# Causal attention: row maxima from full banks, one mask per diagonal bank, two weighted sums in a row

## The reference, cut to what matters

```
x: (8, 1024, 256)                          # batch, positions, features; 16 heads of 16
q, k, v = einsum('bte,hed->bhtd', x, Wq), ... Wk, ... Wv
scores  = einsum('bhtd,bhsd->bhts', q, k)
scores  = where(causal, scores, -inf) / sqrt(256)
w       = softmax(scores, axis=-1)
out     = einsum('bhts,bhsd->bhtd', w, v)
```

## Time and profile before

| | us |
|---|---|
| median of 3 runs | 5277.7 |
| lowest and highest | 5261.9, 5290.58 |
| the profiled execution, whole | 5293.36 |
| its span | 5291.6 |

### The profile page before, as it was taken

How to read it: one execution, slowest core, us unless ns; L and a number is a source line. 1 busy time by engine, 2 the same in 40 slices (tenths; PEclk the granted TensorE clock), 3 DMA queues, 4 the chain that set the end, 5 groups by cost and what they waited for, 6 DMA issues and landing times. The chain is left out here.

```text
span 5291.6 us, 68269 instructions
## 1 busy us (share of the span) xinstructions
PE 4637.5 (88%) x23444; PEld 2457.6 (46%) x23444; DVE 3439.4 (65%) x6212; ACT 2705.4 (51%) x3205; POOL 1377.1 (26%) x1043
## 2 busy tenths in 40 slices
PE   5999999999976888888888888888878999999999
PEld 3544444444433544455445544555543444444443
DVE  5566566656647888878887888455545565565653
ACT  1444444445453344443444344122227888888888
POOL 1011111111112332233233332000004545455454
PEclk7787778778787998999899899999989999999999
DMA  6233222322310000000000000000016766666664
GB/s 166 60 74 64 73 62 62 86 62 72 72 37 15 0 0 0 0 0 0 0 0 0 0 0 0 13 1 0 0 31 156 162 153 144 162 146 154 152 146 110
DMA packets 145900, 322.06 MB, mean 61 GB/s; under 512 B 39504, under 2 KB 64480, under 8 KB 129264
## 3 DMA queue, kind: packets, MB, share of 16 engines
q1 hardware_dynamic: 137664, 310.88, 25.6%
q10 hardware_dynamic: 7920, 7.87, 0.5%
q0 software_dynamic: 64, 0.05, 0.0%
HBM read 237.93 MB, written 80.74 MB: 60 GB/s over the span
## 5 line engine op out<-in xcount | busy, mean ns | idle before, releaser
L1714 ACT ACTIVATE gelu_out<-hidden,b_col 128x1024 f32<-128x1024 f32 x1024 | 1085.4, 1111 | 171.1 <-PE hidden L1628 169.9
L529 ACT ACTIVATE probsT<-scoresT 128x1024 f32<-128x1024 f32 (+3 forms) x768 | 603.8, 810 | 609.7 <-PE scoresT L467 603.9
L577 DVE TENSOR_REDUCE maxima<-front 128x1 f32<-128x512 f32 (+3 forms) x1280 | 735.7, 630 | 274.4 <-PE front L439 177.7
L1694 POOL TENSOR_TENSOR combined<-combined,gated 128x512 f32<-128x512 f32 x480 | 615.6, 1283 | 679.0 <-DVE gated L1812 679.0
L918 POOL TENSOR_TENSOR pair_sums<-sims 128x1024 f32<-128x1024 f32 x256 | 487.9, 1913 | 1140.0 <-DVE pair_exp L1032 777.3
L1812 DVE SCALAR_TENSOR_TENSOR gated<-expert_out,b_col,gates_spread 128x512 f32<-128x512 f32 x480 | 359.1, 748 | 452.1 <-PE expert_out L1638 246.7
L1628 PE MATMUL hidden<-slice_stack,w_stack 128*128 128x512 f32 x2048 | 626.9, 428 | 14.1 <-ACT gelu_out L1714 14.1
L433 PE MATMUL front<-k_stack,q_stack 48*128 48x512 f32 (+3 forms) x1536 | 541.3, 493 | 62.2 <-DVE maxima L577 35.6
L1638 PE MATMUL expert_out<-gelu_out,w_sb 128*32 128x512 f32 x4096 | 547.2, 606 | 31.1 <-DVE gated L1812 26.0
L379 POOL TENSOR_SCALAR_AFFINE_SELECT probsT<-probsT 128x512 f32<-128x512 f32 x256 | 164.7, 644 | 1383.0 <-ACT probsT L529 1383.0
L1628 PEld LDWEIGHTS hidden<-slice_stack,w_stack 128*128 128x128 f32 x2048 | 353.2, 189 | 368.5 <-ACT gelu_out L1714 278.8
(11 more groups left out here) (188 smaller groups left out, 6389.8 us busy)
## 6 DMA issues: line engine op xcount, KB each, us to landing
gates_spread<-gate_scratch SPq DMA_DIRECT2D x512, 256.0 KB, 4.9
stack_scratch<-split_parts SPq DMA_DIRECT2D x192, 256.0 KB, 3.1
slice_stack<-slice_scratch SPq DMA_DIRECT2D x128, 256.0 KB, 7.9
q_stack<-stack_scratch SPq DMA_DIRECT2D x64, 384.0 KB, 6.4
k_stack<-stack_scratch SPq DMA_DIRECT2D x64, 384.0 KB, 9.5
slice_scratch<-slice_parts SPq DMA_DIRECT2D x32, 512.0 KB, 6.3
x_tiles<-in_L_attn_x SPq DMA_DIRECT2D x8, 1024.0 KB, 11.8
out_x<-x_tiles ACTq DMA_DIRECT2D x15, 512.0 KB, 4.7
```

The lines of the kernel that those rows point to most:

```text
L529: nc.scalar.activation(PT[:, i % NPT, 2 * pr:2 * pr + 2, at:BANK], ST[pr][:, :, at:BANK], ACT.Exp, scale=SCALE).then_inc(probs_ready, 1)
L577: nc.vector.tensor_reduce(dst, F[k % 3][:, 0:parts * w].rearrange("p (a k) -> p a k", a=parts), AX.X, ALU.max)\
L1694: nc.gpsimd.tensor_tensor(CM[:, par, hc, :], CM[:, par, hc, :], Y[:, u % 2, :], ALU.add)\
L1714: nc.scalar.activation(GH[:, k % 4, :, :], HP[k % HPB][:, :, :], ACT.Gelu, bias=b1c[:, u % E:u % E + 1])\
```

## The change

- `MAXB` now lists nine units a head, all of 512 columns: WHOLE, four of one query tile by four key blocks, as before; DIAGS, two banks with the four 128 x 128 diagonal blocks of a query half; MIXED, three banks that join the unmasked rests (1 + 3, 1 + 3 and 2 + 2 blocks). No unmasked piece carries a mask any more.
- A DIAGS bank is first filled by one bfloat16 matmul of the identity with the mask repeated four times (L428, 128 rows, 512 columns), and the four blocks are added onto it. The two half masks, their GpSimd work and two small DMAs at the start go.
- DIAGS and MIXED units of a pair are issued together: unit e = 0 waits for the banks of both heads, then the pieces go head 0, head 1, head 0, head 1. The WHOLE units stay one by one.
- A unit's cost in the order is 0.6, whatever its kind.
- `maxima` has eight slots for each query tile and is shared by the groups; the last step of a group is a reduction of 256 elements a partition in place of a maximum of two times 32.
- The sums of two groups are issued one after the other, behind the scores of every second group.

```diff
-    MAXB = [((4, 0),), ((0, 0), (4, 1)), ((5, 0),), ((1, 0), (5, 1)), ((6, 0),), ((2, 0),), ((7, 0),), ((6, 1),),
-            ((3, 0),), ((7, 1),)]
+    WHOLE = [[(qt, 0, 4)] for qt in range(4, KT)]
+    DIAGS = [[(qt, qt, 1) for qt in (4 * c, 4 * c + 2, 4 * c + 1, 4 * c + 3)] for c in range(2)]
+    MIXED = [[(1, 0, 1), (3, 0, 3)], [(5, 4, 1), (7, 4, 3)], [(2, 0, 2), (6, 4, 2)]]
+    MAXB = [WHOLE[0], DIAGS[0], WHOLE[1], MIXED[0], WHOLE[2], DIAGS[1], WHOLE[3], MIXED[1], MIXED[2]]
...
-            return 0.06 + len(MAXB[u[4]]) * width(*MAXB[u[4]][0]) / 960
+            return 0.6
...
-            if NG * n + i >= LAG:
-                pieces.append((("v", NG * n + i - LAG), 0.2))
+            if i % 2 == 1 and NG * n + i > LAG:
+                pieces += [(("v", NG * n + i - LAG - 1), 0.2), (("v", NG * n + i - LAG), 0.2)]
...
-                bank_free(k)
-                w = width(*MAXB[i][0])
-                half = slice(64 * e, 64 * (e + 1))
-                for a, (qt, kc) in enumerate(MAXB[i]):
-                    diag = kc == qt // 4
-                    at = (a + 1) * w
-                    mm = nc.tensor.matmul(F[k % 3][:, a * w:at], QS[rows, hf, q, qt * P:(qt + 1) * P],
-                                          KS[rows, hf, q, kc * BANK:kc * BANK + w], start=True, stop=not diag,
-                                          tile_position=(64 * e, 0))
-                    if diag:
-                        nc.tensor.matmul(F[k % 3][:, at - P:at], IH[half, 0, :], MH[half, :], start=False, stop=False,
-                                         tile_position=(64 * e, 0))
-                        mm = nc.tensor.matmul(F[k % 3][:, at - 64:at], IH[half, 1, :], MH[half, 0:64], start=False,
-                                              stop=True, tile_position=(64 * e, 0))
-                mm.then_inc(front_done, 1)
+                if len(MAXB[i]) == 1:
+                    bank_free(k)
+                    k -= e
+                    piece(0, e, *MAXB[i][0], start=True, stop=True).then_inc(front_done, 1)
+                elif e == 0:
+                    bank_free(k)
+                    bank_free(k + 1)
+                    diag = len(MAXB[i]) == 4
+                    if diag:
+                        for e in range(2):
+                            nc.tensor.matmul(F[(k + e) % 3][:, :], identb[:, :], MK[:, :].unsqueeze(1).to_broadcast([P, 4, P]),
+                                             start=True, stop=False)
+                    at = 0
+                    for qt, first, blocks in MAXB[i]:
+                        last = at + blocks == 4
+                        for e in range(2):
+                            mm = piece(at, e, qt, first, blocks, start=not diag, stop=not diag or last)
+                            if last:
+                                mm.then_inc(front_done, 1)
+                        at += blocks
...
-                    nc.vector.tensor_tensor(NM[:, g, :].rearrange("p (h t) -> p h t", h=G), both[:, :, :, 0],
-                                            both[:, :, :, 1], ALU.max).then_inc(rowmax_ready, 1)
+                    nc.vector.tensor_reduce(NM[:, g, :].rearrange("p (h c b) -> p h b c", c=2, b=2),
+                                            M2[:, :, :, :].rearrange("p h (a b c) s -> p (h a) b c s", a=2, b=2),
+                                            AX.X, ALU.max).then_inc(rowmax_ready, 1)
+                    dve.drain()
```

More of the change, by code:

```diff
@@ L246, in causal_attention @@
         XN = sb("xn", [P, 2, D])
-        M2 = sb("maxima", [P, HH, 2 * KT])
+        M2 = sb("maxima", [P, G, KT, KT])
         NM = sb("row_max", [P, 2, G * KT])
@@ L548, in _ @@
         def _(dve):
-            nc.vector.memset(M2[:, :, :], -3e38)
+            nc.vector.memset(M2[:, :, :, :], -3e38)
             dve.drain()
```

55 lines of the change are left out of this document (27 added, 28 removed).

## The result

| | before | after |
|---|---|---|
| median, us | 5277.8 (4 runs, 5261.9 to 5290.6) | 5435.8 (4 runs, 5431.4 to 5446.4) |
| span of the profiled execution | 5291.6 | 5438.0 |
| ratio of the runs, with 95% interval | | 1.0304 (1.0271 to 1.0336) |

The change makes the kernel 158 us slower, and the spans of the two profiled executions differ by 146.4. That is 56 us above the top of the forecast range. The page of the changed kernel answers the earlier trace rows: TensorE is busy for a smaller share, 86%, and its granted clock stays in the sevens for twelve slices.

The account below looks back on a forecast made before the run. TensorE's work in the attention, bank passing with VectorE and the clock were taken to decide. TensorE's work +35, opening +12, ScalarE +8 and clock -42 gave +13: 5306 us profiled, 5291 against the median; range 5180 to 5380.

Parts of the forecast that it names:

- rival C: Attention maxima: VectorE runs dry at DIAGS pairs and the clock stays as it is; +80 us, 5358, chance 0.28.
- opening: Before the first scores: eight DIAGS pairs waiting for two of three banks leave VectorE idle; +12 us (0 to 15).
- small masks out, mask banks in, with their 112 full stretches: Maxima: 1024 blocks' small masks go, -106; 256 mask matmuls come, +94; 112 more full-tiling stretches at 0.23 us each.
- pieces of 128 columns for pieces of 512: Maxima: per pair set two 512-column pairs go, eight of 128 come; +50 us, or -12 if loads were hidden.
- the wait for two banks, in the steps: Maxima within the steps: other work lies between them, so the forecast takes nothing for it.
- doubled sums: tiling and ScalarE's cover: Weighted sums: 117 fewer column-tiled stretches at 0.25 us each, against +8 us for ScalarE's lost cover.
- the clock: Attention: TensorE's half-clock share goes from 44% to 36%; -42 us (0 to -84).
- The rise: Attention: two sums together are 3.7 us of dense work, so the clock should rise from half more often.
- The fall: Attention: between doubled sums lie longer stretches without a sum, on which the clock may fall more often; no size given.
- 530 us of slack in 1400: Attention: VectorE's idle time, given as the argument against rival C.
- a cover that ScalarE loses: Scores behind every second group wait for a buffer ScalarE still reads, some 80 wide double groups; +8 us (0 to 16).
- tiling changes saved: Weighted sums: column-tiled stretches fall from 382 to 265, each saving 0.25 us of leaving and entering.

Follow-up runs that it names:

- e12: e5 with the mask banks undone: two small half-row masks behind each diagonal block, head after head; 5435.1 us, 1.0314 of before.
- e5: The changed kernel with single sums and each unit waiting for its own bank alone, MIXED units head after head; 5249.5 us, 0.9941 of before.
- e6: The changed kernel with each unit waiting for its own bank alone as in e5, doubled sums kept; 5308.1 us, 1.0050 of before.
- e1: The kernel before with one edit, the weighted sums of two groups issued together; 5276.2 us, 1.0002 of before.
- e2: The changed kernel with the weighted sums issued one by one again; 5285.7 us, 1.0009 of before.
- e10: The changed kernel with a weighted sum counted as 0.8 in place of 0.2 when fills are placed, same instructions; 5304.9 us, 1.0051 of before.
- e7: The kernel before with VectorE reducing only a quarter of each piece (left out work); 4985.1 us, 0.9440 of before.
- e14: The changed kernel with each of the 256 mask matmuls made twice, same result; 5493.7 us, 1.0388 of before.
- e4: The changed kernel without the 256 mask matmuls (left out work); 5311.9 us, 1.0054 of before.
- e3: The kernel before with diagonal-piece units issued for both heads together, piece by piece, after both banks are free; 5328.6 us, 1.0079 of before.
- e13: e7 with the sums doubled as in e1 (left out work); 4996.5 us, 0.9450 of before.

## Why the prediction was wrong

The median came out at 5435.8 against the 5291 forecast, above the range and above rival C. The prediction weighted its prices by the half share of before, so what is measured at equal clock is put on the same footing by the factor 1433.9/1207 = 1.188; the clock's row is then what is left of the steps (1561.1 - 1.188 x 1264). Edit by edit, in us (each row is rounded by itself):

| term | forecast | measured | from |
|---|---|---|---|
| opening | +12 | +16 | traces of before and after |
| small masks out, mask banks in, with their 112 full stretches | -106 + 94 + 26 = +14 | -61 | e12 to e5, 51 x 1.188 |
| pieces of 128 columns for pieces of 512 | +50 | +65 | before to e12, 55 x 1.188 |
| the wait for two banks, in the steps | 0 | +33 | e6 to after, 27.5 x 1.188 |
| doubled sums: tiling and ScalarE's cover | -29 + 8 = -21 | +30 | e5 to e6, 25.5 x 1.188 |
| the clock | -42 | +59 | half share 42% to 51% |
| after the attention, and the earlier start | 0 | +3 | traces |
| sum | +13 | +146 | |

**The clock is the step that failed**, by 101 of the 133 us. The prediction wrote "I take the half share from 44% to 36%", and over the steps it went from 42% to 51%. Both things that it weighed are in the trace. TensorE in order of time, in the stretches whose clock stands in the first section:

```profile
740.69 3.64 PE L478 MATMUL pv<-probsT,values 128*32 128x512 f32 x16
744.26 0.58 PE L463 MATMUL scoresT<-q_stack,k_stack 50*128 50x256 f32 x2
...
746.63 1.71 PE L478 MATMUL pv<-probsT,values 128*32 128x512 f32 x16
748.28 0.50 PE L463 MATMUL scoresT<-q_stack,k_stack 50*128 50x512 f32 x2
...
749.80 0.49 PE L414 MATMUL front<-k_stack,q_stack 48*128 48x512 f32 x1 [0.55 <-DVE maxima L583]
...
751.08 0.59 PE L428 MATMUL front<-mask_query_major,ident_bf 128*128 128x512 bf16 x2 [0.56 <-DVE maxima L583]
```

This is one episode; the sums over all of them stand above. A double sum runs at half from 740.69, and at 745.17 the clock rises. The next double sum takes 1.71 us at the full clock. Then come scores and maxima without a sum, twice held by VectorE, and at 751.99 the clock falls again. The rise was counted on. The fall was named in the same paragraph and given no number. In the kernel before, the rise wins (e1, 121 us fewer at half); with the new banks the fall does (e5 to e6, 110 us more), and with the two-bank wait as well by far more (e2 to after, 370). Neither edit alone on the kernel before would have told it. The stretches of before do show what came ahead of a rise and of a fall, but not how many of each the new order would have. What could have been read from them is the size: the range left no room for a half share above 44%, though each percent is worth 5 us (1434 x 0.01 x 0.375) and the stage had seen both levels under the same kinds of work.

The Trainium skill, "TensorE: Matmul & The Clock Gate", Why this matters for your kernels, advises against idle gaps of TensorE in mid-kernel. The gaps here are 0.55 and 0.56 us ahead of this fall, far shorter than those that the page speaks of, so it doesn't settle this case. On average TensorE does idle longer ahead of a fall than ahead of a rise (1.2 and 0.1 of 5 us), but idle time doesn't rank the kernels. In their steps e2 and e10 idle for 9% and 10% with 30% at half, and e12 and before for 4% with 45% and 42%.

**Banks and VectorE.** "Within the steps other work lies between the maxima, and the forecast takes nothing for it" failed by 33 us. Rival C had the mechanism, VectorE kept dry and TensorE then kept waiting, with 25 us for it and the clock unchanged. So C was right in kind and nearly in size, and fell short of the time by what the clock and the doubled sums added. That VectorE has 530 us of slack in 1400, which was held against C, is no evidence: VectorE idles because banks come late, and with quarter reductions the steps lose 286 us all the same (e7; 100 of them at equal clock, the rest by the clock). The opening was right in kind. VectorE idles 1.65 us ahead of each DIAGS pair (1.8 forecast), and 0.46 ahead of each MIXED pair, which wasn't priced; 8 and 12 of these, less 2, make 17.

**TensorE's work.** The forecast of masks, pieces and their tiling was +64, measured +5. The swap of the masks has the wrong sign. The mask bank was about right: 0.24 was its price at the full clock, and a second one costs 0.28 of the steps at equal clock (e14). Its change of tiling was priced too high: e4 gives 0.29 for a bank together with it (70 us for 240), and start to start a bank with it takes 0.27 at the full clock and 0.47 at half, where the prices gave 0.36 and 0.65. The small masks were too cheap. If the 70 us of the banks in e4 hold in e5 too, they cost 70 + 51 = 121 us at equal clock for the 960 blocks of the steps, 0.13 each, where the row of before showed 0.09 from start to start. So the time from one start to the next was not all that they cost; what the rest is, no run shows. The pieces came out at +65 against +50, although a pair of 128 columns took 0.12 in place of 0.16; part of the +65 must be something else that the new `MAXB` brings, and isn't told apart.

**Doubled sums.** The prediction had the wait, a cover that ScalarE loses, and too small: 15 to 22 us in three pairs of kernels, where 8 were forecast (80 x 0.56 x 0.2 is 9, to be exact). The larger part of the miss is the 29 us for tiling changes saved, which can't be seen. The Trainium skill, "TensorEngine Tiling (Array Packing)", Key Properties, has every change of tiling mode drain TensorE, which spoke for this edit; it comes out at +21 to +28 at equal clock with 117 column-tiled stretches fewer, so whatever the drains gave back was outweighed; no run here isolates them.

One reading of the profile in the prediction is off without bearing on it: TensorE's 88% are over three times GpSimd's 26%, not twice.

**Still open.** (a) How an order of work sets the half share: three orders show its price, and the traces what came ahead of each rise and fall, but none of it would have given 51% beforehand. (b) The 7 to 12 us that every kernel with the new `MAXB` spends after the attention, in layers whose instructions are the same; e1, e3, e7 and e13 don't have them. (c) Why the doubled sums cost 28, 21 and 25 us at equal clock with whole reductions and 12 with short ones.

## What to carry to other kernels

A change that moves work on an engine whose clock changes by stages should be priced in two columns, the us at equal clock and the us at half, and timed with every edit by itself: here the edit with the good idea (full banks, one mask matmul for four blocks) was worth 0.6%, and two companions that looked free turned it into a loss of 3%. Where three buffers pass between two engines, look at a producer that waits for two of them: here it gave the consumer an idle spell each time, however much slack its busy share showed. Before reordering for a fine reason, try two or three trivial reorderings of the same instructions; their scatter (131 us here) is what a forecast of the order has to beat.

## What the runs showed of the hardware that was not expected

- The same 8110 matmuls in another order take 5305, 5394 or 5436 us, and the difference lies in the granted clock: 30%, 47% and 51% of the steps at 1.2 GHz.
- A busier TensorE isn't granted more. It is at half for 42% of the time when busy for 96% of the steps (before), for 9% when busy for 97% (e7), and for 30% when busy for 90% (e10). What e7 changed was VectorE's work alone.
- The level depends on the kind of work. In the 5 us ahead of a rise TensorE spent 3.9 us on the full or column-tiled array, ahead of a fall 1.6, with row-tiled matmuls and 1.2 us of idle time for the rest (after, 66 rises and 65 falls).
- Work added to TensorE can be paid back in part by the clock: a second mask bank costs 68 us at equal clock, and 38 us fewer lie at half (e14). All four executions of e14 have a higher mean clock (0.882 to 0.885) than all four of the changed kernel (0.876 to 0.880). Without any masks (e4) it is still at half for 46% of the steps.
- Four row-tiled pairs of 128 float32 columns take 0.49 us at the full clock and 0.92 at half, 0.12 and 0.23 each, when they follow each other without a mask between.
